# Moving the residual of x1 into an accumulating DMA and its statistics to ScalarE, with a looser order of the steps

## The reference

```
q = layernorm(x);  k = v = ctx
gates from [q, k, v] -> a 256 x 256 decay matrix D for each head
C = (q k^T / sqrt(32)) * D;  h = C v / (max(|sum C|, exp(-max)) + eps)
hn = (h - mean) * rsqrt(var + eps)  for each row and head;  hn = hn * ln_scale
x1 = x + hn
z  = layernorm(x1)                       # mean and variance over the 512
gate, up = mx(z) @ mx(w_gate)^T, mx(z) @ mx(w_up)^T
out = x1 + mx(silu(gate) * up) @ mx(w_down)^T
```

## Time and profile before

| | us |
|---|---|
| median of 3 runs | 546.87 (544.37 and 546.87, and one of 1383.94) |
| the profiled execution | 548.92 |
| its span, first to last instruction | 547.0 |
| busy: PE, DVE, ACT, POOL | 449.5, 434.3, 243.2, 249.9 |

### The profile page before, as it was taken

How to read it: one execution, slowest core, us unless ns; L and a number is a source line. 1 busy time by engine, 2 the same in 40 slices (tenths; PEclk the granted TensorE clock), 3 DMA queues, 4 the chain that set the end, 5 groups by cost and what they waited for, 6 DMA issues and landing times.

```text
span 547.0 us, 10343 instructions
## 1 busy us (share of the span) xinstructions
PE 449.5 (82%) x3465; PEld 299.6 (55%) x3465; DVE 434.3 (79%) x615; ACT 243.2 (44%) x341; POOL 249.9 (46%) x228
## 2 busy tenths in 40 slices
PE   0697988399778686959789698799799999999993
PEld 0597988168556465657658384344344444444441
DVE  5569886679798897979789876798978888888781
ACT  1656663246354363726264464244344434434431
POOL 2444541232553537264644564755334353354443
PEclk9997885579978797987859577799989999999999
DMA  7455621143231413141420203011111111111211
GB/s 225 155 185 168 224 98 38 42 120 116 84 114 59 140 59 120 24 146 48 131 67 20 77 2 116 1 38 40 38 40 40 68 47 38 38 38 39 76 38 38
DMA packets 30566, 43.73 MB, mean 80 GB/s; under 512 B 6980, under 2 KB 11972, under 8 KB 30532
## 3 DMA queue, kind: packets, MB, share of 16 engines
q1 hardware_dynamic: 27280, 42.80, 23.8%
q10 hardware_dynamic: 3252, 0.46, 0.5%
HBM read 34.41 MB, written 8.85 MB: 79 GB/s over the span
## 4 chain that ended last, share of the span: by engine, by line
PE 42%; issue 18%; POOL 17%; DVE 13%; ACT 4%; DMA 3%; POOLq 1%; SPq 0%; DVEq 0%; ACTq 0%
PE psA L1359 8%; PE psA L1368 8%; PE psC L1386 7%; PE psC L1193 4%; POOL early L615 3%; PE psB L1378 3%; PE psA L1256 2%; PE psC L1236 2%; DMA early<-in_x_dram 2%; POOL wq L552 2%; POOL kTa L678 2%; POOL xc L648 2%; PE psA L1165 2%; DVE qTa L1128 2%; DVE pam L941 2%
## 5 line engine op out<-in xcount | busy, mean ns | idle before, releaser
L678 POOL TENSOR_TENSOR kTa<-kTa,ps 128x1024 bf16<-128x1024 bf16 x32 | 62.0, 1937 | 100.8 <-DVE kTa L1131 100.8
L1284 PE MATMUL psA<-vp,DC 128*128 128x128 f32 x512 | 72.4, 309 | 12.1 <-DVE DC L1035 12.1
L1284 PEld LDWEIGHTS psA<-vp,DC 128*128 128x128 f32 x512 | 70.1, 223 | 14.1 <-issue 14.1
L552 POOL TENSOR_TENSOR wq<-wq,ws 128x1024 bf16<-128x1024 bf16 x24 | 50.6, 2108 | 51.9 <-DVE wq L969 51.9
L1359 PE MATMUL psA<-WgT,qTa 128*128 128x512 bf16 x256 | 64.7, 399 | 2.5 <-ACT hf L823 2.5
L1368 PE MATMUL psA<-WuT,qTa 128*128 128x512 bf16 x256 | 63.1, 391 | 1.2 <-DVE kTa L1119 1.2
L1386 PE MATMUL psC<-WdT,kTa 128*128 128x512 bf16 x256 | 60.5, 379 | 2.4 <-ACT kTa L888 2.4
L888 ACT ACTIVATE kTa<-psB 128x1024 bf16<-128x1024 bf16 x32 | 32.8, 1024 | 58.1 <-PE psB L1378 57.9
L1119 DVE TENSOR_TENSOR kTa<-kTa,psA 128x1024 f32<-128x1024 f32 x32 | 39.0, 1219 | 19.4 <-PE psA L1368 19.4
L1035 DVE SCALAR_TENSOR_TENSOR DC<-psA,DC 128x512 f32<-128x512 f32 x64 | 41.0, 684 | 13.5 <-ACT DC L814 10.7
L814 ACT ACTIVATE DC<-psB 128x512 f32<-128x512 f32 x64 | 37.2, 597 | 20.1 <-PE psB L1270 19.6
(11 more groups left out here) (132 smaller groups left out, 857.8 us busy)
## 6 DMA issues: line engine op xcount, KB each, us to landing
early<-in_x_dram SPq DMA_DIRECT2D x16, 512.0 KB, 4.0
wraw<-in_L_ffn_w_down_dram SPq DMA_DIRECT2D x8, 512.0 KB, 5.6
early<-in_ctx_dram SPq DMA_DIRECT2D x8, 512.0 KB, 4.8
wraw<-in_L_ffn_w_gate_dram SPq DMA_DIRECT2D x8, 512.0 KB, 4.3
wraw<-in_L_ffn_w_up_dram SPq DMA_DIRECT2D x8, 512.0 KB, 3.4
x_scratch<-early SPq DMA_DIRECT2D x8, 512.0 KB, 3.0
kTa<-x_scratch SPq DMA_DIRECT2D x16, 256.0 KB, 2.7
out_dram<-kTa SPq DMA_DIRECT2D x16, 256.0 KB, 2.0
```

The source lines that it names most:

```text
L552: nc.gpsimd.tensor_tensor(blocks(wq[p][:, :]), blocks(wq[p][:, :]), spread(ws4[p][:, :], UB), ALU.mult).then_inc(wq_ready.sem, 1)
L678: nc.gpsimd.tensor_tensor(blocks(pd[h]), blocks(pc[h]), spread(ps4[h][:, :], PB), ALU.mult).then_inc(pq_ready.sem, 1)
L1284: last = nc.tensor.matmul(psA[:, j, to:to + P], DC[n % DCN][:, i4 * P:(i4 + 1) * P], values[:, left:left + P], start=i4 == 0, stop=c == 0, ...
```

## The change

- **Residual.** POOL's two passes go, and so do the load of the second x and its buffer. PE turns the 32 roots of each row (`root_transpose`), ACT copies them (`copy_root`), and two float32 matmuls with a 32 x 512 table that holds ln_scale on its block diagonal (`scale_root`) put root times ln_scale, spread over 512 columns, into psC[1] and psC[0]. DVE multiplies the heads with it in two instructions straight into x1, and a DMA issued from POOL adds x to x1 in place.
- **Statistics.** In steps 1 to 7 `x1_stats` on DVE is replaced by `x1_sums` on ACT: a Copy with a summed output, a small instruction for the negated mean, and a Square with bias and a summed output, each pass twice (once for each 128 rows). Batch 7 keeps the DVE statistics.
- **Order.** x1 of batch b-1 is summed at the end of step b, and normalised, rounded, scaled back and transposed in step b+1. So batch 6 joins batch 7 in the third stage, where their pieces are spread over tiles 1 to 9 (DVE: pairs 0 to 7). ACT now does `x1_norm` first in a step, `evac_gate_up` unit 0 after exps 5, `head_power` after `copy_state`, and `square`, `evac_xq`, `evac_gate_up` unit 1, `x1_sums` last. PE does its `w_transpose` after decay 5 and at the very end of a step, behind `x_transpose`, and the root work just ahead of heads 4 to 7. The last power on POOL (L609) is cut in two and put behind `back_p`.

```diff
 POOL
+            def residual(b):
+                gp.wait_ge(hn_ready.sem, hn_ready.at(b, 2))
+                gp.dma_start(x1, x_v[b], accum_op=ALU.add).then_inc(x_added, 16)
+            def x1_rsqrt_sums(b):
+                gp.wait_ge(mv2_ready.sem, mv2_ready.at(b, 1))
...
+                ch.link(nc.gpsimd.tensor_scalar(rt2[:, :], sums[1], 1.0 / E, LN_EPS, ALU.mult, ALU.add))
+                ch.link(nc.gpsimd.tensor_tensor(rs2[:, :], rt2[:, :], mhalf[:, 0:NCH], ALU.pow))
+                nc.gpsimd.tensor_tensor(nb2[:, :], nm2[:, :], rs2[:, :], ALU.mult)
 step: head_rsqrt(b-1), w_back(unit 1), back_x(b-2), carry_q(b+1), residual(b-1),
       w_back(next unit 0), x1_rsqrt_sums(b-1), weigh(b+1)
 ACT
+            def copy_root(b):
+                nc.scalar.activation(rT[:, :], psC[1][0:DROW, 0:NCH * P], ACT.Copy)
+            def x1_sums(b):
+                act.wait_ge(x_added, 16 * b + 16)
+                for c in range(NCH):
+                    last = nc.scalar.activation(xn[:, c, :], x1[:, c, :], ACT.Copy, accum_out=sums[0][:, c:c + 1])
+                ch.link(last)
+                ch.link(nc.scalar.activation(nm2[:, :], sums[0], ACT.Copy, scale=-1.0 / E))
+                for c in range(NCH):
+                    last = nc.scalar.activation(xn[:, c, :], x1[:, c, :], ACT.Square, bias=nm2[:, c:c + 1],
+                                                accum_out=sums[1][:, c:c + 1])
+                last.then_inc(mv2_ready.sem, 1)
 step: x1_norm(b-2), copy_h(b,0), exps 4, 5, evac_gate_up(0), copy_v, copy_state, head_power(b-1),
       exps 6, 7, copy_root(b-1), round_const, copy_h(b,1), exps 0, 1 of b+1, copy_v, exps 2, 3,
       square(b), evac_xq(b-2), evac_gate_up(1), x1_sums(b-1), round_const
 DVE
+            def head_norm(b, p, c, bank):
+                ve.wait_ge(r_mm.sem, r_mm.at(b, c + 1))
...
+                nc.vector.tensor_tensor(x1[:, c]..., hf[p][:, c, :, 0:DH], psC[bank]..., ALU.mult)
 step: c_mult 0-3, w_front(0), head_var(b-1), w_round(1), x1_round(b-2), c_mult 4-7, w_pow(0),
       head_norm(b-1) twice, w_front(1), w_round(0), w_pow(1)
 PE
+            def root_transpose(b):
+                for c in range(NCH):
+                    last = nc.tensor.transpose(psC[1][0:DROW, c * P:(c + 1) * P], root[:, c * NH:c * NH + DROW], ident[:, :])
+            def scale_root(b, c, bank):
+                nc.tensor.matmul(psC[bank][:, :], rT[:, c * P:(c + 1) * P], ltab[:, :], start=True, stop=True)
 step: heads 0-3, decay 4, 5, w_transpose(0), centre(1), qk(1), state, decay 6, 7,
       root_transpose(b-1), scale_root twice, heads 4-7, inter, decay 0, qk(0), decay 1, centre(0),
       decay 2, 3 of b+1, x_transpose(b-2), w_transpose(1)
```

More of the change, by code:

```diff
@@ L199, in bass_mlstm_cross_attention__mx_ffn_kernel @@
         mv2 = sb("mv2", [P, NCH, 2])
+        sums = [mv2[:, :, k] for k in range(2)]
         rs2 = sb("rs2", [P, NCH])
@@ L651, in step @@
             def step(b, p, n, first, last):
+                second = isinstance(b, int) and b == 1
                 if not first:
                     head_rsqrt(b - 1)
+                w_back(2 * b + B + 1, 1)
+                if not (first or second):
+                    back_x(b - 2)
+                if not last:
+                    carry_q(b + 1, 1 - p)
                 if not first:
@@ L844, in step @@
             def step(b, p, n, first, last):
-                evac_gate_up(2 * b + B, 0, b)
-                if not first:
-                    head_power(b - 1)
+                second = isinstance(b, int) and b == 1
+                if not (first or second):
+                    x1_norm(b - 2)
                 copy_h(b, p, 0)
@@ L850, in step @@
                 exps(b, 5)
+                evac_gate_up(2 * b + B, 0, b)
                 copy_v(b, p, 1)
-                if not first and not (isinstance(b, int) and b == 1):
-                    evac_xq(b - 2)
                 copy_state(b, p)
+                if not first:
+                    head_power(b - 1)
                 exps(b, 6)
                 exps(b, 7)
+                if not first:
+                    copy_root(b - 1)
                 if not last:
                     round_const(2 * b + B + 2, 0)
-                if not first:
-                    x1_norm(b - 1)
                 copy_h(b, p, 1)
-                evac_gate_up(2 * b + B + 1, 1, b)
                 if not last:
@@ L869, in step @@
                 square(b, p)
+                if not (first or second):
+                    evac_xq(b - 2)
+                evac_gate_up(2 * b + B + 1, 1, b)
+                if not first:
+                    x1_sums(b - 1)
                 if not last:
@@ L1088, in step @@
                     c_mult(b, k)
+                if not last:
+                    w_front(2 * b + B + 2, 0, b + B // 2 + 1)
                 if not first:
                     head_var(b - 1, 1 - p)
-                if not last:
-                    w_front(2 * b + B + 2, 0, b + B // 2 + 1)
                 w_round(2 * b + B + 1, 1)
-                if not first:
-                    head_norm(b - 1, 1 - p)
+                if not (first or isinstance(b, int) and b == 1):
+                    x1_round(b - 2)
                 for k in range(HPC, 2 * HPC):
@@ L1100, in step @@
                 if not first:
-                    x1_stats(b - 1)
+                    head_norm(b - 1, 1 - p, 0, 1)
+                    head_norm(b - 1, 1 - p, 1, 0)
                 if not last:
@@ L1104, in step @@
                     w_round(2 * b + B + 2, 0)
-                if not first:
-                    x1_round(b - 1)
-                if not last:
                     w_pow(2 * b + B + 3, 1)
-            pipeline(ch, ve, step)
-            head_var(B - 1, 1)
+            pipeline2(ch, ve, step)
             fch = Chain(ve, dve_ffn_step, 2 * FFN_LINKS)
```

236 lines of the change are left out of this document (146 added, 90 removed).

## The result

| | before | after |
|---|---|---|
| median of the runs, us | 545.65 (4 runs) | 578.81 (4 runs, 574.63 to 586.67) |
| ratio | | 1.059, 95% interval 1.0504 to 1.0677 |
| profiled execution, its span, us | 548.92, 547.0 | 578.07, 576.4 |
| a step, mean of four (`copy_h`(2,1) to `copy_h`(6,1)), us | 30.5 | 34.0 |
| first gate to the end of the span (stage 3), us | 212.1 | 221.2 |

One of the runs of before (1383.94) is far off all others; it and one slow run of the changed kernel (586.67) are left out of the ratio. The forecast was 542, with a range of 529 to 558. The largest rival was 566.

The account below looks back on a forecast made before the run. It took a loop through ACT, PE and POOL, its terms summing to 29.1 us a step, to bound the changed kernel. Third-stage terms 3.8 + 5.1 - 4.4, rounded with rests to 4.8 us gained, gave 546.87 - 4.8 = 542 us, range 529 to 558.

Parts of the forecast that it names:

- the loop: In each steady step, from one `x1_norm` to the next through ACT, PE and POOL: sets the step at 29.1 us.
- the third rival: In the steps, the DMA adding x lands beyond 13 us behind its issue; at 17 us, 566 us; chance 0.05.
- the first rival: In the steps, the loop on ACT doesn't close and DVE stays the bound: 26.3 us each, 528 us; chance 0.20.
- The one wait of DVE of 2 to 3 us: Sign in each step: DVE waits 2 to 3 us before `x1_round` or c_mult 4 to 7, released by ACT.
- `scale_root` twice 1.9: On the loop, PE: two float32 matmuls of 512 columns, taken at 0.95 us each.
- Heads 4 to 7, 3.73: On the loop, PE behind `scale_root`: the matmuls of heads 4 to 7 take 3.73 us.
- the second rival: On the loop, TensorE's clock is low: a step of 33.6 us, the kernel 565 us; chance 0.18.
- four in a row: On the loop, PE ahead of the root: four idles in a row, PE's longest idle being about 1.9 us.
- POOL's root at 1.27: Last term of the loop, behind `x1_sums`: POOL makes the root in 1.27 us.
- root work and waits: Third stage, tiles 1 and 2, PE: two matmuls 1.9 us, some 1.3 waiting for the power's second half.
- Each piece fits DVE's slack: Third stage, rounding two batches: the lower bound, 0 us, against an upper bound of 10; 4 was taken.
- the page against the change: In the steps: a skill page says DVE's two-port passes block POOL-issued DMA descriptors, moving the landing by those passes' length.

Follow-up runs that it names:

- e1: The changed kernel with throw-away matmuls filling idle TensorE ahead of the root transposes and the second `w_transpose`: 572.9 us, ratio 1.0447.
- e9: The changed kernel, steps left as they are, with batch 7's root made before the third stage as in e7: 569.45 us, ratio 1.0459.
- e4: The kernel before, with only POOL's second pass and SP's second load replaced by the accumulating DMA: 566.16 us, ratio 1.0363.
- e5: The kernel before, with only the statistics of x1 moved from DVE to ScalarE: 551.94 us, ratio 1.0121.
- e2: The changed kernel with heads 4 to 7 ahead of the root work in PE's queue: 554.27 us, ratio 1.0114.
- e6: e2 plus throw-away matmuls ahead of `centre` of the second half and of the second `w_transpose`: 552.9 us, ratio 1.0135.
- e7: e2 with batch 7's root made by ScalarE and POOL before the third stage, replacing the two last powers: 543.01 us, ratio 0.9953.

## Why the prediction was wrong

The span grew by 29.4 us where 4.8 less was predicted. From `copy_h`(0,1) to the first gate the kernel before took 207.1, the changed one 230.6 (355.2 less 124.6), and 200.1 was predicted; the third stage grew by 9.1 and not by 2.2. So 30.5 of the miss lies in the steps and 6.9 behind them, less 3.2 by which this execution's step 0 was early.

**Right: that the loop sets the step.** Its terms, predicted and as measured from 229.37 to 263.15:

| term | predicted | measured |
|---|---|---|
| `x1_norm` to the root made by POOL | 7.2 | 7.05 |
| root transposes, `copy_root`, hand-overs | 1.1 | 1.26 |
| `scale_root` twice | 1.9 | 3.71 |
| heads 4 to 7 | 3.73 | 6.05 |
| `inter`, hand-over | 1.2 | 1.16 |
| `copy_h` to `square` | 5.36 | 5.37 |
| `square` to `x1_sums` | 3.8 | 3.69 |
| `x1_sums` | 3.6 | 3.34 |
| POOL's root, to the next `x1_norm` | 1.2 | 2.15 |
| sum | 29.1 | 33.8 |

Six of the nine terms are good to 0.3 us. Right as well: DVE's 25.1 us, the DMA hidden (the third rival false here), ACT not running ahead (the first rival false), heads 4 to 7 released by `scale_root`, and 4.4 us from `copy_h`(7,1) to the first gate (4.3). The one wait of DVE of 2 to 3 us, named as a sign, came as several: 1.78 for ACT's `round_const`, 1.18 and 0.79 for `scale_root`, 2.11 for `qk`. One reading was off: "DVE has 3 us more work than any other engine" holds for the first stretch of the earlier trace rows only (26.43 against 23.90); in the second PE has 25.68 against DVE's 25.71.

**Wrong: the two terms "`scale_root` twice 1.9" and "Heads 4 to 7, 3.73".** Both were taken at 2.4 GHz, and they ran at 1.2: in full (3.78 and 6.0 to 6.4) in four of the five steps from `x1_norm`(0) on and in the part step behind them, and from 171.2 on in the first (3.24 and 5.84). That is the second rival, at 0.18. Its 33.6 us a step was nearly the measured one, but in part by luck: `qk` and `centre`, for which it had 1.8 us, ran fast, heads lost 2.3 and not 1.6, `scale_root` 1.8 and not 1.1, and 0.9 of POOL's root was not in it. e1 shows it in both directions: with these terms at the high clock the step is 30.0, which is 29.1 plus what POOL's root was off. What the prediction set against the rival was that PE's longest single idle on the loop (1.9) stays under the 2.61 that had come before a slow row. The trace has the fall behind idles of 0.99 and 1.15 us and within one of 0.98. The prediction had named four in a row there and given them little weight. Five steps and the part step behind them, at 4.7 each, are 28 of the 30.5 us.

**Wrong: POOL's root at 1.27.** Its last small instruction took 1.05 instead of the 0.20 of the earlier trace rows, in each step, beside DVE's L1013 (261.84, 1.23 long), and 0.20 at 359.40 in the changed kernel, where DVE idled. The row was from the end of step 7; in the steps of the kernel before the same instruction had taken 0.54 to 0.88, so the trace at hand had shown the term too small:

```profile
243.53 0.61 POOL L547 TENSOR_TENSOR nb<-nm,rs 128x2 f32<-128x2 f32 x1
```

The Trainium skill, page "SBUF — State Buffer", section "SBUF: two separate sides", says that the loser between VectorE and GpSimd is blocked for the other's whole instruction, also where VectorE's has two SBUF inputs and GpSimd's reads SBUF. The rows agree: L1013, which has two, ends at 263.07 and POOL's at 263.12. That is 0.9 us on the loop, since the order puts the two side by side every time; the earlier trace rows had the same effect the other way round, DVE's 1.39 beside POOL's L648.

**Wrong: the third stage, in two terms.** Up to tile 2 the sum had 3.2 us for root work and waits; it is 4.9 more than before. Cut in two (2.90 and 3.01), the powers stand between `back_p` that PE waits for, the root transposes wait for the second, and DVE waits 4.85 for `scale_root` in turn; e9 takes 9.2 off this part. From tile 2 on the sum had 0.7 less than before, by taking 4 for rounding two batches where the upper bound was 10; it came out 4.2 more, so 4 should have been about 9. "Each piece fits DVE's slack" was the wrong end to be near. That part was measured in two kernels (4.2 and 5.3) but not taken apart.

**The DMA.** The section on the page against the change ended with no row for a DMA issued from POOL. Now there are some: it lands in 5.6 us (median), the plain load of the same x, in the first stage of the same kernel, in 3.4, and POOL's issue takes 1.27. So a blocked issue did not show as more than 2.2 us in the median; how much of these is the adding and how much the issue isn't separated.

**The range.** It stopped at half of rival 2, though that rival's full size was 565 and nothing spoke for half of it. The 14 us beyond 565 are the third stage (6.9), the part step behind the five periods, which is as slow as they are (4.6), step 1, 2.4 longer than predicted, and small terms of both signs.

**Why the change didn't pay as meant.** Both halves take work from DVE, the busiest engine of the earlier trace rows. e4 and e5 show that neither pays alone in the old order, and e2 that together with the new order they do: its steps take 29.8 against 30.5, though its third stage gives more back. The new order alone, without the two halves, was not run. What spoiled it was one detail of that order, the root work ahead of heads 4 to 7 in PE's queue.

## What to carry to other kernels

When work is moved off the busiest engine, write down the loop that it joins, from one instruction to the same instruction of the next step, and put each engine's work that is not needed there behind what is: moving the root work behind heads 4 to 7 gave back 24 of 33 us. Price TensorE's terms on such a loop twice, at 1.2 and at 2.4 GHz, and give the low one a real chance where several idles of about 1 us stand ahead of them: here it came in most such steps, though e6 has one where it didn't. Look at the hand-written end of a pipeline by itself: here it held 8 us that no steady step shows (e7, e9), and in the kernel before perhaps 4 (29.6 against e9's 25.3 up to tile 2; not tried there).

## What the runs showed of the hardware

- TensorE's granted clock fell to 0.50 behind idles of 0.99 and 1.15 us, 0.4 us into one of 0.98, and stayed there for 10 us in which the engine was busy for 8.9. In each of the last five steps of the changed kernel it fell within the third such idle (the three were 0.69 to 1.19 us long). In e6 idles of 1.00, 1.14 and 0.37 us had no fall behind them.
- A float32 matmul of 512 columns, with 32 rows of weights, takes 0.98 us at the high clock and 1.89 at the low one (1.96 to 1.98 and 3.78 for two of them, which the trace has as four records).
- The read of ScalarE's accumulator is a row of 0.19 us behind each pass with a summed output. The next pass starts 0.09 after that row's start, so two sums of 128 x 512 by Copy end 1.3 us after their start. The Square passes took 0.72 each, the Copy passes 0.62.
- An accumulating DMA of 512 KB issued by POOL lands in 5.6 us, 5.8 in e4.
